# Attention row maxima from half-depth products: two query tiles side by side in the two row halves of the array, one VectorE maximum for both

## The chip, the cores and the metric

The kernel runs on one NeuronCore of a Trainium2 chip. The metric is device time in microseconds (us) for one launch; lower is better. All matrix work is on TensorE (PE), and "weight load" is its LDWEIGHTS (PEld), which the profile lists apart. VectorE is DVE, ScalarE is ACT, GpSimd is POOL, and the queue that issues nearly all transfers is SP.

## The reference

A block of two layers over x of shape (8, 1024, 512): attention (8 heads of 64, biases drawn at random) and then a gated feed-forward layer. Only the attention matters here.

```python
qk = x @ W_qk + b_qk                       # x is layer-normalised before
q, k = qk.reshape(b, s, H, D_HEAD, 2)[..., 0], qk.reshape(...)[..., 1]
v = (x @ W_v + b_v).reshape(b, s, H, D_HEAD)
sim = einsum('bihd,bjhd->bhij', q, k) * D_HEAD ** -0.5
attn = softmax(sim, axis=-1)               # over all 1024 keys j
o = einsum('bhij,bjhd->bihd', attn, v).reshape(b, s, V_DIM)
y = _layernorm(o @ W_out + b_out, ln_gamma, ln_beta)
return (y + x) * RSQRT2
```

## The kernel before

The program has two passes, attention (to about 2,040 us) and then the output projection with the feed-forward layer, which the change does not touch. The attention pass goes through 8 batches of 8 heads, one head at a time. Matmuls that need accuracy take fp32 numbers split into a high part and a low part in the type fp32r.

For each head, `qA` holds the high part of q twice: partitions 0 to 63 come from ACT (L555), and partitions 64 to 127 are a copy made by a DMA (L206). `kA` holds the low part of k in partitions 0 to 63 (DVE, L380) and its high part in 64 to 127 (ACT, L554). `kB` holds a second copy of the high part of k in partitions 0 to 63, by the DMA issued right behind (L207), and a row of ones in partition 64. `qB` holds the low part of q (DVE, L382) and in partition 64 the negated row maxima.

Softmax needs for each query the maximum over all keys before the exponentials are made. So the scores are computed twice:

- "Rows": `rows(b, h, first, end)` on PE (L683 to L701) makes 16 products of 128 queries by 512 keys, each over 128 partitions (q high times k low plus q high times k high), into two PSUM banks in turn (`ps_max[0]`, `ps_max[1]`). `reduce_max` on DVE (L389) takes the maximum of each bank. Product j waits for the maximum of product j-2. After the 16th, `join_max` joins the halves, PE turns the 128 x 8 result (L706), ACT copies it out (L560) and a DMA puts it in `qB`.
- "Scores": `scores` (L708 to L722) makes the transposed scores with the maxima already taken off, four matmuls for each of 8 key tiles: L720 over 128 partitions and L721 over 65. ACT takes the exponential (L578), and POOL adds up the probabilities (L305).
- `p_at_v` (L724) multiplies four key tiles of probabilities by v. These matmuls are fp32, each with 64 stationary columns: the two query halves go to the two column halves of the array. `sum_rows` (L737) has the same form.

The order on every engine is written by hand. While head h has its scores and p_at_v, head h+1 has its rows, and the projection of q and k (`project_qk`, two halves of 512 queries with 12 matmuls each, L661) is spread among them: the second half for h+1 early in the head, the first half for h+2 late. There are four kinds of head on PE and DVE: `late_v_head` (place 0, with the second half of v's projections), `plain_head` (places 1 to 5, and place 6 of the last batch), `turning_head` (place 6, with the transposes of the next batch's input) and `early_v_head` (place 7). `begin_head` runs the last four tiles of p_at_v of the head before, `sum_rows` and `turn_max`.

On SP, `copy_qk(b, h+1, half)` waits for ACT's `qk_hi_done` and issues the copy of q and then that of k. In before, `rows` waits for the copy of q (`q_dup_in`) and for DVE's low part of k (`k_lo_done`); only `scores`, a whole head later, waits for the copy of k (`k_dup_in`).

`project_v` of tile t needs the bank `ps_misc` emptied of tile t-1: PE waits in `free_of_v` for DVE's `store_v` (L387), which stands in DVE's order among the maxima.

The PE order of a plain head, 16 products of rows among the rest:

```python
project_qk(b, h + 1, 1, 8, 12); rows(b, h + 1, 2, 3)
scores(b, h, 0, 1); rows(b, h + 1, 3, 4); scores(b, h, 1, 3)
rows(b, h + 1, 4, 6); scores(b, h, 3, 4); rows(b, h + 1, 6, 8)
```

Of the kernel before, what the change touches and what calls it, by code (L numbers as in the profile page):

```python
# [17 lines left out]
F32 = mybir.dt.float32  # L18
# [28 lines left out]
def rows_of(j):  # L47

    if j < 8:
        return j % 4, j // 4  # L50
    return 4 + (j - 8) // 2, j % 2


def attention_pass(nc, x, w_qk, b_qk, w_v, b_v, w_out, w_r, w_out_raw, stage, o_scratch, inv_scratch, ln1_stats, ident):
    with ExitStack() as ctx:
# [48 lines left out]
        ps_max = [ctx.enter_context(nc.psum_tensor(f"ps_max{i}", [P, HALF], F32)) for i in range(2)]  # L104
# [4 lines left out]
        first_turns = [misc4] + [ps[:, :].rearrange("p (k n) -> p k n", k=KC) for ps in (ps_max[0], ps_max[1], ps_o)]  # L109
# [63 lines left out]
        def turn_bank(t):  # L173

            bank = ps_misc if t in (4, 5, 6) else ps_max[1] if t in (1, 3) else ps_max[0]
            return bank[:, :].rearrange("p (k n) -> p k n", k=KC)
# [5 lines left out]
        with nc.Block() as block:  # L182
# [160 lines left out]
            def _(dve):  # L343
# [45 lines left out]
                def reduce_max(b, h, first, end):  # L389

                    for j in range(first, end):
                        r, kh = rows_of(j)
                        dve.wait_ge(rows_done, 128 * b + 16 * h + j + 1)
                        dve.tensor_reduce(half_max[:, r, kh:kh + 1], ps_max[(j + 1) % 2][:, :], AX_X,  # L394
                                          ALU.max).then_inc(max_done, 1)

                def join_max(b, h):

                    dve.wait_ge(max_done, 128 * b + 16 * h + 16)
                    dve.tensor_reduce(neg_max[:, :], half_max[:, :, :], AX_X, ALU.max, negate=True).then_inc(neg_max_done, 1)  # L400
# [20 lines left out]
                for t in range(4):  # L421
                    reduce_max(0, 0, 3 * t, 3 * t + 3)
                    store_v(0, t)
                reduce_max(0, 0, 12, 16)
                join_max(0, 0)

                def plain_head(b, h, last):
# [10 lines left out]
                    reduce_max(b, h + 1, 0, 3)  # L438
                    store_qk_lo(b, h + 1, 1)
                    reduce_max(b, h + 1, 3, 4)  # L440
                    if h >= 1:
                        invert_sums(b, h - 1)
                    reduce_max(b, h + 1, 4, 10)
# [4 lines left out]
                    reduce_max(b, h + 1, 10, 16)  # L448
                    join_max(b, h + 1)

                def late_v_head(b, h):
                    bb = b + h // HEADS
                    store_qk_lo(b, h + 1, 0)
                    reduce_max(b, h + 1, 0, 3)
                    store_qk_lo(b, h + 1, 1)
                    reduce_max(b, h + 1, 3, 4)
                    if h >= 1:
                        invert_sums(b, h - 1)
                    reduce_max(b, h + 1, 4, 7)
                    store_v(bb, 4)  # L460
                    reduce_max(b, h + 1, 7, 9)
                    store_v(bb, 5)
                    reduce_max(b, h + 1, 9, 10)
                    store_v(bb, 6)
                    reduce_max(b, h + 1, 10, 12)
                    store_v(bb, 7)
                    reduce_max(b, h + 1, 12, 16)
                    join_max(b, h + 1)

                def turning_head(b, h):  # L470
# [8 lines left out]
                    reduce_max(b, h + 1, 0, 2)  # L479
                    store_xT_lo(b + 1, 4, turn_bank(4))  # L480
                    reduce_max(b, h + 1, 2, 4)
                    invert_sums(b, h - 1)
                    reduce_max(b, h + 1, 4, 5)
                    store_xT_lo(b + 1, 5, turn_bank(5))
                    reduce_max(b, h + 1, 5, 7)
                    normalise(b + 1, 6)
                    normalise(b + 1, 7)
                    reduce_max(b, h + 1, 7, 16)
                    join_max(b, h + 1)

                def early_v_head(b, h):
# [6 lines left out]
                    reduce_max(b, h + 1, 1, 7)  # L498
                    store_v(b + 1, 0)
                    reduce_max(b, h + 1, 7, 9)  # L500
                    store_v(b + 1, 1)
                    reduce_max(b, h + 1, 9, 11)
                    store_v(b + 1, 2)
                    reduce_max(b, h + 1, 11, 13)
                    store_v(b + 1, 3)
                    reduce_max(b, h + 1, 13, 16)
# [23 lines left out]
                dve.reciprocal(xhat[0][:, :], ps_max[1][:, :]).then_inc(recip_done, 1)  # L530
# [5 lines left out]
            def _(act):  # L536
# [21 lines left out]
                def store_max_row(b, h):  # L558
                    act.wait_ge(max_turned, 8 * b + h + 1)
                    act.activation(max_row[:, :], ps_max[0][0:TT, 0:P], ACT.Copy).then_inc(max_row_done, 1)  # L560

                def store_o(b, h):
# [4 lines left out]
                    act.activation(sums[:, :], ps_max[1][:, :], ACT.Copy).then_inc(sum_copied, 1)  # L567
# [80 lines left out]
            def _(pe):  # L648
# [34 lines left out]
                def rows(b, h, first, end):  # L683

                    for j in range(first, end):
                        r, kh = rows_of(j)
                        if j == 0:
                            pe.wait_ge(q_dup_in[0], 128 * b + 16 * h + 16)
                            pe.wait_ge(k_lo_done, 16 * b + 2 * h + 1)
                            if h >= 2:  # L690
                                pe.wait_ge(sum_copied, 8 * b + h - 1)
                        if j == 1 and h >= 1:
                            pe.wait_ge(max_row_done, 8 * b + h)
                        if j == 4:
                            pe.wait_ge(k_lo_done, 16 * b + 2 * h + 2)
                        if j == 8:
                            pe.wait_ge(q_dup_in[1], 128 * b + 16 * h + 16)
                        if j >= 2:
                            pe.wait_ge(max_done, 128 * b + 16 * h + j - 1)
                        pe.matmul(ps_max[(j + 1) % 2][:, :], qA[h % 2][:, r * P:(r + 1) * P],  # L700
                                  kA[h % 2][:, kh * HALF:(kh + 1) * HALF], start=True, stop=True).then_inc(rows_done, 1)  # L701

                def turn_max(b, h):

                    pe.wait_ge(neg_max_done, 8 * b + h + 1)
                    pe.transpose(ps_max[0][0:TT, 0:P], neg_max[:, :], ident[:, :]).then_inc(max_turned, 1)  # L706
# [30 lines left out]
                def sum_rows(b, h, all_max):  # L737
# [3 lines left out]
                    for half in range(2):  # L741
                        ins = pe.matmul(ps_max[1][half * DH:(half + 1) * DH, :], ones[:, :],
# [15 lines left out]
                for t in range(4):  # L758
                    rows(0, 0, 3 * t, 3 * t + 3)
                    project_v(0, t)  # L760
                rows(0, 0, 12, 14)
                free_of_qk(0, 0, 0)
                project_qk(0, 1, 0, 0, 12)
# [719 lines left out]
```

## Time and profile before

| what | us |
|---|---|
| median of 3 runs | 2854.5 (2852.35 to 2860.09) |
| profiled execution, device time | 2849.87 |
| its span, first to last instruction | 2848.1 |
| PE busy | 2670.5 (94% of the span) |
| DVE busy | 1782.4 (63%) |
| POOL busy | 1425.2 (50%) |
| ACT busy | 1258.6 (44%) |

The profiled execution lies 1.77 us above its own span. Busy time of PE is a union of records whose ends are modelled, so it says only that PE seldom rests; what a matmul really takes is read from the distance between two starts.

### The profile page before, as it was taken

Reading aid. Unit: us, or ns where it says so; the run is one execution under the profiler, and the core shown is the slowest. Engines: PE = TensorE matmul, PEld = TensorE weight load, DVE = VectorE, ACT = ScalarE, POOL = GpSimd, SP = SyncE. Lnnn points to the kernel's source line nnn. Section 1 sums busy time; section 2 is a strip of 40 time slices with the busy share of each in tenths; the row PEclk is TensorE's granted clock in tenths of the full one; section 3 lists DMA queues with packets and bytes.
Section 4 is the critical chain, followed back from the end, with each engine's and each line's share of the span. In section 5 each row is a group of like instructions: output and inputs, shape, how many; then the busy total and the mean of one; then the engine's idle time right before and its main releaser. Section 6 shows DMA issues by size and latency. Waiting matters only on the chain. (4 is left out here: it accounts for less than half of the span.)

```text
span 2848.1 us, 35993 instructions
## 1 busy us (share of the span) xinstructions
PE 2670.5 (94%) x11376; PEld 1800.3 (63%) x11376; DVE 1782.4 (63%) x2761; ACT 1258.6 (44%) x1719; POOL 1425.2 (50%) x738
## 2 busy tenths in 40 slices
PE   5998999999899999989999998999679999999999
PEld 4655655565565566656556565665357777777777
DVE  5556456546645654564565456455388787878785
ACT  2444244334434433443443344344355565556554
POOL 2575466557545655754565565466523333333333
PEclk9999999999999999999999999999889999999999
DMA  3211021121112112111211211112212121212110
GB/s 104 59 38 36 23 72 34 30 64 40 34 25 75 31 30 65 42 34 27 75 31 30 65 42 34 27 45 68 85 53 74 58 75 57 75 57 75 55 64 30
DMA packets 89739, 145.06 MB, mean 51 GB/s; under 512 B 20096, under 2 KB 20608, under 8 KB 89600
## 3 DMA queue, kind: packets, MB, share of 16 engines
q1 hardware_dynamic: 89600, 143.19, 17.6%
q8 instruction: 90, 1.47, 0.2%
q14 instruction: 49, 0.40, 0.0%
HBM read 75.24 MB, written 33.81 MB: 38 GB/s over the span
## 5 line engine op out<-in xcount | busy, mean ns | idle before, releaser
L305 POOL TENSOR_TENSOR acc<-acc,probs 128x1024 f32<-128x1024 f32 x384 | 915.1, 2383 | 215.8 <-ACT probs L578 187.1
L394 DVE TENSOR_REDUCE half_max<-ps_max 128x1 f32<-128x512 f32 x1024 | 678.7, 686 | 517.1 <-PE ps_max L700 511.3
L578 ACT ACTIVATE probs<-ps_st 128x1024 f32<-128x1024 f32 x512 | 522.2, 1024 | 702.4 <-PE ps_st L721 677.0
L732 PE MATMUL ps_o<-probs,v 128*64 128x512 f32 x2048 | 474.2, 605 | 12.9 <-issue 12.9
L301 POOL TENSOR_TENSOR acc<-probs 128x1024 f32<-128x1024 f32 x64 | 157.4, 2460 | 626.4 <-ACT probs L578 626.4
L700 PE MATMUL ps_max<-kA,qA 128*128 128x512 f32 x1024 | 394.6, 425 | 66.3 <-DVE half_max L394 51.1
L720 PE MATMUL ps_st<-qA,kA 128*128 128x512 f32 x1024 | 419.7, 410 | 7.7 <-DMA qB<-max_row 2.4
L721 PE MATMUL ps_st<-qB,kB 65*128 65x512 f32 x1024 | 412.7, 403 | 0.0
L700 PEld LDWEIGHTS ps_max<-kA,qA 128*128 128x128 f32 x1024 | 192.4, 192 | 207.2 <-DVE half_max L394 95.9
L732 PEld LDWEIGHTS ps_o<-probs,v 128*64 128x64 f32 x2048 | 137.4, 138 | 284.5 <-issue 256.2
L720 PEld LDWEIGHTS ps_st<-qA,kA 128*128 128x128 f32 x1024 | 197.4, 193 | 76.0 <-ACT probs L578 33.5
L721 PEld LDWEIGHTS ps_st<-qB,kB 65*128 65x128 f32 x1024 | 197.9, 193 | 41.9
L661 PE MATMUL ps_misc<-xT_hi,wqk_lo 128*128 128x512 f32 x508 | 209.8, 413 | 5.0 <-DVE v L387 2.2
L661 PE MATMUL ps_misc<-xT_lo,wqk_hi 128*128 128x512 f32 x508 | 205.4, 404 | 0.0
L661 PE MATMUL ps_misc<-xT_hi,wqk_hi 128*128 128x512 f32 x508 | 204.6, 403 | 0.0
L554 ACT ACTIVATE kA<-ps_misc,bqk 64x512 fp32r<-64x512 f32 x127 | 86.6, 682 | 228.7 <-PE ps_misc L661 226.2
L387 DVE TENSOR_TENSOR v<-ps_misc,bv 128x512 f32<-128x512 f32 x60 | 41.5, 691 | 187.5 <-PE ps_misc L669 187.5
L380 DVE SCALAR_TENSOR_TENSOR kA<-ps_misc,bqk,kA 64x512 fp32r<-64x512 f32 x127 | 95.9, 755 | 91.1 <-ACT qA L555 73.5
L1385 PE MATMUL bank<-mix_wout_hi,o_lo 128*128 128x512 f32 x256 | 103.5, 404 | 24.1 <-DVE o_lo L1166 14.7
L560 ACT ACTIVATE max_row<-ps_max 8x128 fp32r<-8x128 f32 x64 | 17.1, 268 | 244.0 <-PE ps_max L706 244.0
L661 PEld LDWEIGHTS ps_misc<-xT_hi,wqk_lo 128*128 128x128 f32 x508 | 98.2, 193 | 26.1 <-DVE v L387 5.3
L661 PEld LDWEIGHTS ps_misc<-xT_hi,wqk_hi 128*128 128x128 f32 x508 | 98.5, 194 | 23.4
(166 smaller groups left out, 4539.4 us busy)
## 6 DMA issues: line engine op xcount, KB each, us to landing
stage<-in_L_attn_x_dram SPq DMA_DIRECT2D x32, 512.0 KB, 5.7
qA<-qA SPq DMA_DIRECT2D x128, 128.0 KB, 2.2
kB<-kA SPq DMA_DIRECT2D x128, 128.0 KB, 2.3
o_scratch<-oT SPq DMA_DIRECT2D x128, 128.0 KB, 2.3
stage<-o_scratch SPq DMA_DIRECT2D x16, 1024.0 KB, 5.6
xc<-in_L_attn_x_dram SPq DMA_DIRECT2D x16, 1024.0 KB, 5.4
out_dram<-gate SPq DMA_DIRECT2D x64, 256.0 KB, 2.0
inv_cols<-inv_scratch SPq DMA_DIRECT2D x126, 128.0 KB, 2.8
```

Of the source, the lines that this page charges most:

```text
L301: pool.tensor_tensor(acc[:, :], probs[:, 0, :], probs[:, 1, :], ALU.add).then_inc(acc_done, 1)
L305: pool.tensor_tensor(acc[:, :], acc[:, :], probs[:, j, :], ALU.add).then_inc(acc_done, 1)
L380: dve.scalar_tensor_tensor(kA[i][0:DH, cols], ps[DH:P, :], bqk[DH:P, hd:hd + 1], f32(kA[i][DH:P, cols]), ALU.add, ALU.subtract).then_inc(k ...
L394: dve.tensor_reduce(half_max[:, r, kh:kh + 1], ps_max[(j + 1) % 2][:, :], AX_X, ALU.max).then_inc(max_done, 1)
L554: act.activation(kA[i][DH:P, cols], ps[DH:P, :], ACT.Identity, bias=bqk[DH:P, hd:hd + 1])
L578: act.activation(probs[:, j, :], ps_st[j % 2][:, :], ACT.Exp).then_inc(exp_done, 1)
L661: ins = pe.matmul(ps[:, :], w[:, kc, h % HEADS, :, :].rearrange("p s d -> p (s d)"), xt[:, kc, cols], start=(n == 0), stop=(n == 11))
L700: pe.matmul(ps_max[(j + 1) % 2][:, :], qA[h % 2][:, r * P:(r + 1) * P], kA[h % 2][:, kh * HALF:(kh + 1) * HALF], start=True, stop=True).th ...
L720: pe.matmul(ps_st[j % 2][:, cols], kA[h % 2][:, tile], qA[h % 2][:, cols], start=True, stop=False)
L721: ins = pe.matmul(ps_st[j % 2][:, cols], kB[h % 2][:, tile], qB[h % 2][:, cols], start=False, stop=True)
L732: ins = pe.matmul(ps_o[half * DH:(half + 1) * DH, :], v[:, j, hd * DH:(hd + 1) * DH], probs[:, j, half * HALF:(half + 1) * HALF], start=(j ...
L1385: ins = pe.matmul(out, a[:, kc, a_cols], b[:, kc, b_cols], start=(i == 0), stop=(i == len(prods) - 1))
```

## The change

`rows` no longer makes 16 products over 128 partitions. It makes 8 pairs m = 0 to 7. The two matmuls of a pair take 64 partitions each: the first takes partitions 0 to 63 of `qA` and of `kB` for one query tile, the second partitions 64 to 127 of `qA` and `kA` for the next query tile. Both are q high times k high, so the term q high times k low is no longer in the maximum. They write the two banks of one PSUM tensor, `ps_pair`, and one DVE instruction takes both maxima (128 x 2 x 512 in, 128 x 2 out). Pair m waits for the maximum of pair m-1. The waits on `k_lo_done` become waits on `k_dup_in`. In each kind of head the calls are placed anew, on PE and on DVE.

```diff
-def rows_of(j):
-    if j < 8:
-        return j % 4, j // 4
-    return 4 + (j - 8) // 2, j % 2
+def rows_of(m):
+    if m < 4:
+        return 2 * (m % 2), m // 2
+    return 4 + 2 * ((m - 4) // 2), m % 2
...
-        ps_max = [ctx.enter_context(nc.psum_tensor(f"ps_max{i}", [P, HALF], F32)) for i in range(2)]
+        ps_pair = ctx.enter_context(nc.psum_tensor("ps_pair", [P, 2, HALF], F32))
+        ps_max = [ps_pair[:, i, :] for i in range(2)]
...
 def reduce_max(b, h, first, end):
-                    for j in range(first, end):
-                        r, kh = rows_of(j)
-                        dve.wait_ge(rows_done, 128 * b + 16 * h + j + 1)
-                        dve.tensor_reduce(half_max[:, r, kh:kh + 1], ps_max[(j + 1) % 2][:, :], AX_X,
-                                          ALU.max).then_inc(max_done, 1)
+                    for m in range(first, end):
+                        r, kh = rows_of(m)
+                        dve.wait_ge(rows_done, 64 * b + 8 * h + m + 1)
+                        dve.tensor_reduce(half_max[:, r:r + 2, kh], ps_pair[:, :, :], AX_X, ALU.max).then_inc(max_done, 1)
...
-                def rows(b, h, first, end):
+                def rows(b, h, m):
+                    r, kh = rows_of(m)
+                    if m == 0:
+                        pe.wait_ge(q_dup_in[0], 128 * b + 16 * h + 16)
+                        pe.wait_ge(k_dup_in[0], 128 * b + 16 * h + 16)
+                        if h >= 2:
+                            pe.wait_ge(sum_copied, 8 * b + h - 1)
+                        if h >= 1:
                             pe.wait_ge(max_row_done, 8 * b + h)
-                        if j == 4:
-                            pe.wait_ge(k_lo_done, 16 * b + 2 * h + 2)
-                        if j == 8:
-                            pe.wait_ge(q_dup_in[1], 128 * b + 16 * h + 16)
-                        if j >= 2:
-                            pe.wait_ge(max_done, 128 * b + 16 * h + j - 1)
-                        pe.matmul(ps_max[(j + 1) % 2][:, :], qA[h % 2][:, r * P:(r + 1) * P],
-                                  kA[h % 2][:, kh * HALF:(kh + 1) * HALF], start=True, stop=True).then_inc(rows_done, 1)
+                    if m == 2:
+                        pe.wait_ge(k_dup_in[1], 128 * b + 16 * h + 16)
+                    if m == 4:
+                        pe.wait_ge(q_dup_in[1], 128 * b + 16 * h + 16)
+                    if m >= 1:
+                        pe.wait_ge(max_done, 64 * b + 8 * h + m)
+                    cols = slice(kh * HALF, (kh + 1) * HALF)
+                    pe.matmul(ps_pair[:, 0, :], qA[h % 2][0:DH, r * P:(r + 1) * P], kB[h % 2][0:DH, cols],
+                              start=True, stop=True)
+                    pe.matmul(ps_pair[:, 1, :], qA[h % 2][DH:P, (r + 1) * P:(r + 2) * P], kA[h % 2][DH:P, cols],
+                              start=True, stop=True).then_inc(rows_done, 1)
```

The order on PE in the new plain head (the pair numbers are the last arguments of `rows`; project_qk calls are in groups of four matmuls):

```python
project_qk(b, h + 1, 1, 0, 4); rows(b, h + 1, 0); project_qk(b, h + 1, 1, 4, 8)
project_qk(b, h + 1, 1, 8, 12); rows(b, h + 1, 1); scores(b, h, 0, 1); scores(b, h, 1, 3)
rows(b, h + 1, 2); scores(b, h, 3, 4); rows(b, h + 1, 3)
free_of_qk(b, h + 1, 1); project_qk(b, h + 2, 0, 0, 4); scores(b, h, 4, 5)
rows(b, h + 1, 4); scores(b, h, 5, 6); p_at_v(b, h, 0)
rows(b, h + 1, 5); scores(b, h, 6, 7); rows(b, h + 1, 6)
project_qk(b, h + 2, 0, 4, 8); scores(b, h, 7, 8); project_qk(b, h + 2, 0, 8, 12)
rows(b, h + 1, 7)
```

In the late_v head DVE now has `reduce_max` of pair 5 ahead of `store_v(bb, 6)`, where before it had products 10 and 11 behind it:

```diff
-                    reduce_max(b, h + 1, 7, 9)
+                    reduce_max(b, h + 1, 4, 5)
                     store_v(bb, 5)
-                    reduce_max(b, h + 1, 9, 10)
+                    reduce_max(b, h + 1, 5, 6)
                     store_v(bb, 6)
-                    reduce_max(b, h + 1, 10, 12)
+                    reduce_max(b, h + 1, 6, 7)
                     store_v(bb, 7)
-                    reduce_max(b, h + 1, 12, 16)
+                    reduce_max(b, h + 1, 7, 8)
```

and PE there has `scores(5)`, `p_at_v`, `free_of_v(5)`, `project_v(6)`, `rows(5)`, `scores(6)`, `free_of_v(6)`, `project_v(7)`, `rows(6)`, `scores(7)`, `rows(7)`, `free_of_v(7)`. In the turning head DVE's maximum of pair 3 stands behind `normalise` of tiles 6 and 7, and PE has `rows(3)`, `p_at_v`, `rows(4)`. In the early_v head pair 0 is moved behind `scores(0)`, and the last pair ahead of `free_of_v(3)` and the projection. The prologue places its pairs in the same way.

## Rows read from the trace of the kernel before

**Rows 1.** The page: busy time, and the granted clock in 40 slices.

```profile
PE 2670.5 (94%) x11376; PEld 1800.3 (63%) x11376; DVE 1782.4 (63%) x2761; ACT 1258.6 (44%) x1719; POOL 1425.2 (50%) x738
...
PEclk9999999999999999999999999999889999999999
```

**Rows 2.** Groups of instructions, shapes apart: busy us, mean ns of one | idle before.

```profile
L394 DVE TENSOR_REDUCE half_max<-ps_max 128x1 f32<-128x512 f32 x1024 | 678.7, 686 | 517.1 <-PE ps_max L700 511.3
L700 PE MATMUL ps_max<-kA,qA 128*128 128x512 f32 x1024 | 394.6, 425 | 66.3 <-DVE half_max L394 51.1 <-ACT inv_cols L567 8.9 <-DVE xT_lo L373 3.2
...
L1166 DVE TENSOR_TENSOR o_lo<-stage,o_hi 128x2048 fp32r<-128x2048 f32 x16 | 36.5, 2283 | 0.0
...
L1211 DVE TENSOR_TENSOR mr_lo<-stage,mr_hi 128x512 fp32r<-128x512 f32 x64 | 40.8, 698 | 0.0
```

**Rows 3.** Timeline of a late_v head: start us, duration us, engine, instruction.

```profile
837.23 0.40 PE L721 MATMUL ps_st<-qB,kB 65*128 65x512 f32 x1
...
837.47 0.39 PE L700 MATMUL ps_max<-kA,qA 128*128 128x512 f32 x1
...
837.78 0.20 PEld L732 LDWEIGHTS ps_o<-probs,v 128*64 128x64 f32 x4 [0.36 <-issue]
837.79 3.65 PE L732 MATMUL ps_o<-probs,v 128*64 128x512 f32 x16
837.89 0.69 DVE L394 TENSOR_REDUCE half_max<-ps_max 128x1 f32<-128x512 f32 x1 [0.47 <-PE ps_max L700]
838.27 0.14 PEld L732 LDWEIGHTS ps_o<-probs,v 128*64 128x64 f32 x2 [0.29 <-issue]
...
840.41 0.14 PEld L732 LDWEIGHTS ps_o<-probs,v 128*64 128x64 f32 x2 [0.28 <-issue]
841.37 0.19 PEld L669 LDWEIGHTS ps_misc<-wv_hi,xT_lo 128*128 128x128 f32 x1 [0.81 <-issue]
841.37 0.50 PE L669 MATMUL ps_misc<-wv_hi,xT_lo 128*128 128x512 f32 x1
841.48 0.19 PEld L669 LDWEIGHTS ps_misc<-wv_lo,xT_hi 128*128 128x128 f32 x1
841.71 0.40 PE L669 MATMUL ps_misc<-wv_lo,xT_hi 128*128 128x512 f32 x1
```

**Rows 4.** Timeline of a plain head, from the end of its projection on.

```profile
861.27 0.39 PE L661 MATMUL ps_misc<-xT_hi,wqk_hi 128*128 128x512 f32 x1
...
862.39 0.69 ACT L555 ACTIVATE qA<-ps_misc,bqk 64x512 fp32r<-64x512 f32 x1
...
863.66 0.59 SPq L207 DMA_DIRECT2D kB<-kA  x1
...
864.03 0.19 PEld L720 LDWEIGHTS ps_st<-qA,kA 128*128 128x128 f32 x1 [0.48 <-ACT probs L578]
...
864.84 0.19 PEld L700 LDWEIGHTS ps_max<-kA,qA 128*128 128x128 f32 x1
...
865.29 0.19 PEld L700 LDWEIGHTS ps_max<-kA,qA 128*128 128x128 f32 x1 [0.26 <-DVE half_max L394]
```

**Rows 5.** The DMA of L207: landing after issue, us.

```profile
DMA to landing us min/median/max: 2.3/2.3/4.0
```

**Rows 6.** Who waited for whom: us in total, times, longest.

```profile
PEld ps_max L700 <- DVE half_max L394: 95.9, 138, 5.9
...
PE ps_max L700 <- DVE half_max L394: 51.1, 18, 5.4
```

**Rows 7.** Stretches of an early_v head: PE, PEld, DVE, ACT, POOL busy, granted clock, DMA.

```profile
785.00:790.00 5.00, 3.61 (x15) 2.41 (x14) 3.98 (x6) 2.74 (x4) 3.12 (x2) 1.00 0.25 53
790.00:794.00 4.00, 4.00 (x13) 2.05 (x13) 1.39 (x2) 2.05 (x2) 3.92 (x2) 0.57 0.26 70
```

More of the change, by code:

```diff
@@ L566, in store_o @@
                         act.wait_ge(o_done, 8 * b + h)
[L567 removed]
+                    act.activation(sums[:, :], ps_max[1], ACT.Copy).then_inc(sum_copied, 1)
                     act.wait_ge(pv_done, 8 * b + h + 1)
@@ L741, in sum_rows @@
                     for half in range(2):
-                        ins = pe.matmul(ps_max[1][half * DH:(half + 1) * DH, :], ones[:, :],
+                        ins = pe.matmul(ps_pair[half * DH:(half + 1) * DH, 1, :], ones[:, :],
                                         acc[:, half * HALF:(half + 1) * HALF], start=True, stop=True)
@@ L758, in _ @@
                 for t in range(4):
-                    rows(0, 0, 3 * t, 3 * t + 3)
+                    rows(0, 0, t)
                     project_v(0, t)
-                rows(0, 0, 12, 14)
+                rows(0, 0, 4)
                 free_of_qk(0, 0, 0)
-                project_qk(0, 1, 0, 0, 12)
-                rows(0, 0, 14, 16)
+                project_qk(0, 1, 0, 0, 6)
+                rows(0, 0, 5)
+                project_qk(0, 1, 0, 6, 12)
+                rows(0, 0, 6)
+                rows(0, 0, 7)
                 def begin_head(b, h):
@@ L828, in late_v_head @@
                     scores(b, h, 4, 5)
-                    rows(b, h + 1, 7, 9)
+                    rows(b, h + 1, 4)
                     free_of_v(bb, 4)
@@ L832, in late_v_head @@
                     scores(b, h, 5, 6)
-                    rows(b, h + 1, 9, 10)
                     p_at_v(b, h, 0)
@@ L836, in late_v_head @@
                     project_v(bb, 6)
-                    rows(b, h + 1, 10, 12)
+                    rows(b, h + 1, 5)
                     scores(b, h, 6, 7)
@@ L864, in turning_head @@
                     free_of_xhat(b + 1, 3)
-                    rows(b, h + 1, 0, 2)
+                    rows(b, h + 1, 0)
                     free_of_qk(b, h + 1, 1)
@@ L911, in early_v_head @@
                     project_v(b + 1, 0)
-                    rows(b, h + 1, 7, 9)
+                    rows(b, h + 1, 4)
                     scores(b, h, 5, 6)
@@ L915, in early_v_head @@
                     project_v(b + 1, 1)
-                    rows(b, h + 1, 9, 11)
+                    rows(b, h + 1, 5)
                     scores(b, h, 6, 7)
@@ L919, in early_v_head @@
                     project_v(b + 1, 2)
-                    rows(b, h + 1, 11, 13)
+                    rows(b, h + 1, 6)
                     scores(b, h, 7, 8)
```

120 lines of the change are left out of this document (48 added, 72 removed).

## The prediction

> **What bounds the kernel now.** I read the page first. PE is busy 94% of the span, no other engine over 63% [rows 1], and the granted clock is near full in every slice. Then the groups [rows 2]: the row products and their maxima are the two lines that the change rewrites. DVE sits idle 517 us before the maxima, nearly all of it waiting for PE, so a cheaper maximum buys nothing by itself. Last the timelines, where the distance between starts counts. In the run of 128-column fp32r matmuls one takes 0.23 us (841.48 to 841.71) [rows 3]. The attention pass is a chain of such slots on PE with few holes, so the time after is PE's slots plus PE's holes. L700 waited for DVE 147 us in all [rows 6], part of it under a running matmul.
>
> **The row products, if a pair ran at its best.** 1024 products of 0.23 us are 238 us. 512 pairs at one slot each would be 119 us: a gain of 0.23 us a pair, or 1.86 us a head. Whether that comes depends on two things the trace doesn't show for row halves: do both matmuls stream together, and does the array pass freely from whole depth to half depth and back?
>
> The nearest row is p_at_v, which splits the array by columns. Its 16 matmul records take 3.65 us, and a new pair of weight loads starts every 0.43 us (838.27 to 840.41 is five steps) [rows 3]. Two matmuls do run side by side. But the way in and out costs. In: the product of L700 starts at 837.47, so its slot ends at 837.70; the next load starts only at 837.78 and the pair at 838.27 - 0.43 = 837.84, so 0.14 us are lost, of which 0.06 is a load of 64 columns laid bare. Out: the last pair starts at 840.41 + 0.43 = 840.84 and ends at 841.27; the load starts at 841.37 and streaming at 841.48: 0.21 us lost, with 0.11 for 128 columns. With 128-column loads both ways a switch costs about 0.19 to 0.21, say 0.195 us.
>
> The other end is zero. L721 takes 65 partitions of 128 and follows and precedes L720 and L700 without a hole (837.23, 837.47) [rows 3]. But its 65 partitions don't fit a half of the array, so it is no proof that a half-depth matmul is free. I take the switching price, because the new matmuls, like p_at_v, divide the array so that two fit, and L721 doesn't. The Trainium skill ("TensorEngine Tiling (Array Packing)", Tiling Modes, Key Properties) says that changing the tiling mode, not just the tile, drains TensorE. By that rule the half-depth pair pays a drain on each side, as p_at_v does here; without it the sum would be that of the first rival. The trace agrees for columns and shows no case of rows.
>
> Then a pair between whole-depth matmuls costs 0.23 + 2 x 0.195 = 0.62 us against 0.46 before: 0.16 us more. Where one side touches p_at_v, that side's switch was paid already: 0.43 against 0.46, 0.04 less. By the new orders, pairs touching p_at_v are 2 in each of 41 plain heads, 3 in each of 7 turning heads, 1 in each of 7 early_v heads: 110. The other 402 cost 64 us, the 110 give back 4: **+60 us**. Bounds: 512 x -0.23 = -118 us with no drain, and +55 us more (512 x 0.11) if the second load of each pair waits for the first; p_at_v's four loads fall in 0.20 us, so I take them as parallel.
>
> **The wait on the copy of k.** Pair 2 needs `k_dup_in[1]`, where product 4 needed only DVE's low part. Take a plain head and let P = 861.27 be the start of the projection's last matmul [rows 4]. ACT finishes at 863.08, SP issues q's copy and then k's at 863.66, and it lands 2.3 us later [rows 5]: P + 4.69, and some 0.05 to the load. On PE: pair 1 starts at P + 0.43 (slot and switch), scores at P + 0.85, the third scores tile waits for ACT as before (load 864.03, so start P + 2.87), its last matmul is at P + 3.57, and pair 2's load could start at P + 3.89. So PE stands 0.85 us. The next product's load before was at 864.84, already P + 3.57, with the copy still 1.1 us away. Behind this waiting load PE holds scores 3, hence ACT's exponentials, and p_at_v; nothing later in the head has slack on PE to take it up. The late_v head has the same beginning. 49 heads x 0.85: **+42 us**. In turning and early_v heads pair 2 comes later or behind a DVE wait of about the same length. Pair 0 waits for `k_dup_in[0]`, issued about 4 us before; that is free. q's copies were waited for before.
>
> **One buffer instead of two.** Pair m waits for maximum m-1. The new maximum has 1024 elements: from 698 ns at 512 and 2283 ns at 2048 columns [rows 2] one column costs 1.03 ns, so 686 + 512 x 1.03 = 1.21 us. A cycle from load to load: the matmul is over 0.50 us after an exposed load (841.37, 0.50) [rows 3], DVE starts 0.04 us later (837.47 + 0.39 to 837.89), 1.21 us, and 0.05 to PE: 1.81 us. PE's other work between two pairs with n matmuls between fills 0.42 + 0.11 + 0.23n - 0.02 + 0.10, so 1.53 us at n = 4 and 2.47 at n = 8. With n = 4 PE stands 0.28 us. That happens twice in a plain head (pairs 2 to 3 and 5 to 6), once more in the last batch's place 6, twice in late_v (2 to 3, 6 to 7) and twice in turning (2 to 3, 4 to 5): 113 x 0.28 = **+32 us**, and 1 us in the prologue, where pairs 6 and 7 touch. Everywhere else the gap covers it. DVE's own saving (1.21 against two of 0.69 that overlap to about 1.28) is nothing on PE.
>
> **Places on DVE.** In late_v, `store_v` of tile 6 now stands behind the maximum of pair 5. That makes it end 0.54 + 1.13 + 0.69 = 2.37 us after pair 5's load, and PE wants to load for the projection of tile 7 at 1.23 us: 1.1 us late, and some 0.1 at tile 7: 8 heads, **+9 us**. In turning heads pair 4 waits for the maximum of pair 3 behind two `normalise`, 1.3 us, where products 9 and 10 waited 0.65: **+5 us**. Early_v heads lose a wait of 0.4 us behind the last `store_v`: **-3 us**.
>
> **Waits that go.** Back-to-back products in plain heads wait for the maximum two back (865.29 against 865.07 in the free run) [rows 4]: 0.1 to 0.13 us twice and 0.09 at product 0. About 0.3 us in 41 heads and 0.1 in 8: **-13 us**.
>
> **The clock.** A hole can cost more than itself. In the early_v head PE stood 1.7 us before 788.03, and in the stretch from 790 to 794 the granted clock is 0.57 [rows 7], that is about 3.4 us at 1.2 GHz instead of 2.4, which costs 1.7 us. Not every hole did that. The new holes are about 0.9 to 1.1 us. If each of the 49 waits for k drew such a stretch it would be 83 us; if none, nothing. The turning and early_v holes that drew it before stay. I take four new stretches: **+7 us**.
>
> **Sum.** 60 + 42 + 32 + 1 + 9 + 5 - 3 - 13 + 7 = 140. The profiled execution was 2849.9 us, 4.6 below the median of the runs, so 2990. This is 135 us above the median.
>
> **The rivals.**
>
> *No drain.* The pair streams in one slot and costs nothing at the edges. For it: L721's clean passage [rows 3]. Against it: p_at_v's. Then pairs give 118 us back, but PE arrives sooner at both waits: k's copy is 1.34 us away (49 heads, 66 us), and a cycle of 1.82 us between starts meets 0.24 + 0.93 us of work, 0.65 us missing at 113 places (73 us). With 26 for late_v and the other places and -13: +34, so 2884 us. The Trainium skill ("TensorE: Matmul & The Clock Gate", Part 3, Packing small matmuls) has matmuls in distinct row groups start some 4 ns apart. It speaks for the concurrency on which forecast and this rival both build, and says nothing there of what stands around the pair.
>
> *Faster.* The same free pair, and the copy of k is there when pair 2 asks. Place: between L207's landing and pair 2's load. Then the 66 us fall away: -118 + 73 + 26 - 13 = -32, so 2818 us. It decides as soon as a head's new waits are under 1.86 us; in the plain head they are 1.34 + 1.30. Against it: the landing at P + 4.69 hangs on ACT and a 2.3 us transfer, neither of which the change touches.
>
> *Drain, and no full overlap.* Loads one behind the other: 2990 + 55 = 3045. Matmuls one behind the other as well (512 x 0.21 = 109): 3099.
>
> *The change doesn't do what it says.* No drain and no concurrency: 1024 slots as before, k's wait 1.1 us (54), single buffer 0.66 at 113 places (75), 26 and -13: +142, so 2992. It gives the same time as the forecast by another way; the profile would tell them apart.
>
> *Clock.* The new holes draw many slow stretches: up to 83 us more, 3070.
>
> **Chances.** Forecast 0.62; no drain 0.14; faster 0.03; drain without full overlap 0.11; no concurrency and no drain 0.07; clock 0.03. Predicted time 2990. The forecast's own range, with k's wait from 0.6 to 1.1 us and switches from 0.17 to 0.21 us, is 2955 to 3030. The range for 8 in 10 reaches down to the no-drain case and up over the serial loads: 2880 to 3065. What this measurement can tell from no change is 0.3%, about 8.6 us. Faster 0.03, same 0.02 (the no-drain case with half its waits), slower 0.95.
>
> **What would show it.** After: the two matmuls of a pair start within about 10 ns; from a matmul before the pair to the pair's load 0.31 us, and from the pair to the next load again 0.31; an idle PE of 0.8 us before pair 2 in plain heads, ended by the DMA kB<-kA; idle ended by DVE half_max at pairs 3 and 6; a maximum of 1.21 us; a plain head of 28.0 us instead of 26. If the load after a pair starts with the pair, the drain is wrong and the time is near 2884. If the second matmul starts a slot later, concurrency is wrong. If pair 2 is not held by the copy, 42 us are gone.

## Result and profile after

The changed kernel takes **2961.16 us** (2958.14 to 2968.37), against 2853.43 for the kernel before: +107.7 us, ratio **1.0376 [1.035, 1.0402]**. It is slower, as forecast, by 108 us where the forecast had 135. Its profiled span is 2961.5 us, 113.4 more than before; that is what the rows below add up to.

The page after, against [rows 1] and [rows 2]:

```profile
PE 2726.2 (92%) x11376; PEld 1692.5 (57%) x11376; DVE 1716.5 (58%) x2249; ACT 1259.4 (43%) x1719; POOL 1422.4 (48%) x738
...
PEclk9999999999999999999998999999979999999999
...
L395 DVE TENSOR_REDUCE half_max<-ps_pair 128x2 f32<-128x1024 f32 x512 | 626.5, 1224 | 764.7 <-PE ps_pair L699 763.7
...
L697 PE MATMUL ps_pair<-kB,qA 64*128 64x512 f32 x512 | 256.8, 502 | 100.8 <-DVE half_max L395 53.8
...
L699 PE MATMUL ps_pair<-kA,qA 64*128 64x512 f32 x512 | 258.3, 505 | 0.0
```

PE is busy 56 us longer and idle 58 us longer. DVE saves 52 us on the maxima (626.5 against 678.7) and waits 248 us longer for them (764.7 against 517.1): its saving buys nothing. L699 never has an idle time before it, since it starts with L697.

The clearest measure is the distance from one `turn_max` (the 8-row transposes of L706, after L705) to the next, one for each head. Worked out from their starts, mean of the heads of one place, us:

| place | 0 late_v | 1 | 2 | 3 | 4 | 5 | 6 turning | 7 early_v |
|---|---|---|---|---|---|---|---|---|
| before | 37.62 | 28.28 | 25.94 | 25.99 | 25.98 | 33.23 | 29.51 | 42.38 |
| after | 41.10 | 29.72 | 27.92 | 27.86 | 27.87 | 32.20 | 31.15 | 46.15 |
| times heads | +27.8 | +11.5 | +15.8 | +15.0 | +15.1 | **-8.2** | +13.1 | +26.4 |

With -3.4 before the first `turn_max` that is 113 (us, in the profiled executions). After the last one both kernels take 834.1 us. (Place 6 holds the last batch's plain head too, and place 7 has 7 distances.)

A plain head after, from the last matmul of its projection on, as in [rows 4]: start, duration, engine, instruction.

```profile
902.50 0.40 PE L658 MATMUL ps_misc<-xT_hi,wqk_hi 128*128 128x512 f32 x1
902.83 0.49 PE L697 MATMUL ps_pair<-kB,qA 64*128 64x512 f32 x1
902.83 0.49 PE L699 MATMUL ps_pair<-kA,qA 64*128 64x512 f32 x1
903.25 0.50 PE L719 MATMUL ps_st<-qA,kA 128*128 128x512 f32 x1
903.59 0.39 PE L720 MATMUL ps_st<-qB,kB 65*128 65x512 f32 x1
...
905.65 0.50 PE L719 MATMUL ps_st<-qA,kA 128*128 128x512 f32 x1 [0.25 <-ACT probs L575]
...
907.38 0.49 PE L697 MATMUL ps_pair<-kB,qA 64*128 64x512 f32 x1 [0.54 <-DMA kB<-kA]
907.39 0.50 PE L699 MATMUL ps_pair<-kA,qA 64*128 64x512 f32 x1
...
909.20 0.50 PE L697 MATMUL ps_pair<-kB,qA 64*128 64x512 f32 x1 [0.17 <-DVE half_max L395]
```

and PE's weight loads at the first pair:

```profile
902.83 0.18 PEld L697 LDWEIGHTS ps_pair<-kB,qA 64*128 64x128 f32 x1 [0.37 <-issue]
902.83 0.18 PEld L699 LDWEIGHTS ps_pair<-kA,qA 64*128 64x128 f32 x1
903.25 0.19 PEld L719 LDWEIGHTS ps_st<-qA,kA 128*128 128x128 f32 x1 [0.24 <-issue]
903.36 0.19 PEld L720 LDWEIGHTS ps_st<-qB,kB 65*128 65x128 f32 x1
```

The reader sees three things. The pair is one slot: both matmuls and both loads start together. It is fenced off on both sides: 0.33 us from the start of the matmul before to the pair's load, 0.42 from there to the next load, which is bare, that is, under no running matmul (the one behind it comes 0.11 later, when streaming begins). So the pair costs 903.36 - 902.50 - 0.23 = 0.63 us, where two products cost 0.46. And the pair at 907.38 waits for the copy of k, the one at 909.20 for the maximum of the pair before it.

### The profile page after: what moved, and what is told of

It is laid out like the page before. It is cut to its first block and busy times, and to the rows that moved or that the text cites. A ratio compares the mean times of both kernels' runs of the same rounds, so it can differ in the third digit from the quotient of the medians.

```text
span 2961.5 us, 34367 instructions
## 1 busy us (share of the span) xinstructions
PE 2726.2 (92%) x11376; PEld 1692.5 (57%) x11376; DVE 1716.5 (58%) x2249; ACT 1259.4 (43%) x1719; POOL 1422.4 (48%) x738
## 5 line engine op out<-in xcount | busy, mean ns | idle before, releaser
L395 DVE TENSOR_REDUCE half_max<-ps_pair 128x2 f32<-128x1024 f32 x512 | 626.5, 1224 | 764.7 <-PE ps_pair L699 763.7
L731 PE MATMUL ps_o<-probs,v 128*64 128x512 f32 x2048 | 481.2, 613 | 10.5 <-issue 10.5
L719 PE MATMUL ps_st<-qA,kA 128*128 128x512 f32 x1024 | 449.0, 438 | 27.0 <-ACT probs L575 14.6
L697 PE MATMUL ps_pair<-kB,qA 64*128 64x512 f32 x512 | 256.8, 502 | 100.8 <-DVE half_max L395 53.8
L697 PEld LDWEIGHTS ps_pair<-kB,qA 64*128 64x128 f32 x512 | 94.9, 185 | 324.9 <-issue 186.8
L699 PE MATMUL ps_pair<-kA,qA 64*128 64x512 f32 x512 | 258.3, 505 | 0.0
L658 PE MATMUL ps_misc<-xT_hi,wqk_lo 128*128 128x512 f32 x508 | 219.1, 431 | 6.0 <-DVE v L388 2.5
L658 PE MATMUL ps_misc<-xT_lo,wqk_hi 128*128 128x512 f32 x508 | 218.0, 429 | 0.0
L658 PEld LDWEIGHTS ps_misc<-xT_lo,wqk_hi 128*128 128x128 f32 x508 | 99.7, 196 | 38.1 <-issue 24.5
L557 ACT ACTIVATE max_row<-ps_pair 8x128 fp32r<-8x128 f32 x64 | 17.1, 267 | 238.7 <-PE ps_pair L705 238.7
```

The source lines that it names most:

```text
L395: dve.tensor_reduce(half_max[:, r:r + 2, kh], ps_pair[:, :, :], AX_X, ALU.max).then_inc(max_done, 1)
L658: ins = pe.matmul(ps[:, :], w[:, kc, h % HEADS, :, :].rearrange("p s d -> p (s d)"), xt[:, kc, cols], start=(n == 0), stop=(n == 11))
L697: pe.matmul(ps_pair[:, 0, :], qA[h % 2][0:DH, r * P:(r + 1) * P], kB[h % 2][0:DH, cols], start=True, stop=True)
L699: pe.matmul(ps_pair[:, 1, :], qA[h % 2][DH:P, (r + 1) * P:(r + 2) * P], kA[h % 2][DH:P, cols], start=True, stop=True).then_inc(rows_done, 1)
L719: pe.matmul(ps_st[j % 2][:, cols], kA[h % 2][:, tile], qA[h % 2][:, cols], start=True, stop=False)
L731: ins = pe.matmul(ps_o[half * DH:(half + 1) * DH, :], v[:, j, hd * DH:(hd + 1) * DH], probs[:, j, half * HALF:(half + 1) * HALF], start=(j ...
```

## The experiments

Ratios are against the kernel before, timed again with each group of runs: 2852.41 us (half_depth, depth_96, before_k_wait, pair_no_copy), 2855.19 (pair_short_max, pair_k_first and the two spread kernels of experiment 4) and 2855.23 (the last two kernels). Time at the lower clock is added up from the clock records of each kernel's profiled execution; at half the clock, half of such time is lost where PE is busy.

**1. What does half depth cost by itself?** Two kernels made from before. In the first each product uses the upper 64 partitions alone, one at a time; the second takes 96 partitions, which no half of the array can hold.

```diff
-pe.matmul(ps_max[(j + 1) % 2][:, :], qA[h % 2][:, r * P:(r + 1) * P],
-          kA[h % 2][:, kh * HALF:(kh + 1) * HALF], ...)
+pe.matmul(ps_max[(j + 1) % 2][:, :], qA[h % 2][DH:P, r * P:(r + 1) * P],     # half_depth
+          kA[h % 2][DH:P, kh * HALF:(kh + 1) * HALF], ...)
+pe.matmul(ps_max[(j + 1) % 2][:, :], qA[h % 2][0:96, r * P:(r + 1) * P],     # depth_96
+          kA[h % 2][0:96, kh * HALF:(kh + 1) * HALF], ...)
```

> The kernel before with one edit: each of the 16 row products takes only partitions 64 to 127 of qA and kA (q high times k high, so the low part of k is left out of the maxima), one matmul at a time, two buffers and all waits as before. It tells what a half-depth matmul costs by itself. Theory (the array drains on each change between whole and half depth, 0.39 us for a group of products between whole-depth matmuls, 0.195 for one that touches p_at_v): 12 groups in a plain head, about 4.3 us a head, some of it taken up by waits that are there already: 3070 to 3110 us. Rival (half depth is free, as L721's 65 partitions are): 2853 us.

> The kernel before with the row products over partitions 0 to 95 instead of 0 to 127 (the rest of the sum is left out of the maxima). Theory: what costs is the division of the array and not the smaller depth, and 96 partitions don't fit a half, so nothing changes: 2853 us. Rival (any depth below 128 drains): near half_depth's time.

Measured: half depth 3089.68 us, ratio 1.0821 [1.0805, 1.0836], +237 us; a plain head takes 29.55 us instead of 25.98. With 96 partitions 2861.53 us, 1.0031 [1.0018, 1.0043]: all heads of places 0 to 6 keep their length to 0.25 us, and the early_v heads grow (44.28 against 42.38 us, times 7 = 13), by more time at the lower clock (41 us in the seven heads against 14). Of the 237 us of half_depth some 55 are the clock too (245 us at the lower level against 135), but the plain heads of places 2 to 4 have no such time in either kernel, so their 3.6 us are the passages. The loads of half_depth around a group of two products, and the matmuls before and behind it:

```profile
720.93 0.19 PEld L721 LDWEIGHTS ps_st<-qB,kB 65*128 65x128 f32 x1
721.16 0.40 PE L721 MATMUL ps_st<-qB,kB 65*128 65x512 f32 x1
721.49 0.29 PEld L700 LDWEIGHTS ps_max<-kA,qA 64*128 64x128 f32 x2 [0.37 <-issue]
...
722.15 0.19 PEld L720 LDWEIGHTS ps_st<-qA,kA 128*128 128x128 f32 x1 [0.37 <-issue]
...
722.50 0.40 PE L721 MATMUL ps_st<-qB,kB 65*128 65x512 f32 x1
```

From 721.16 to 722.50 are 1.34 us, with four slots of 0.23 in them: 0.41 us lost around the group. Around the pair it is 0.39 (902.50 to 903.59, three slots), so the loss belongs to the two passages and not to what stands between them.

What follows: 65 rows [rows 3] and 96 rows cost nothing at the passage, 64 rows do. Other numbers of rows were not tried. The number of products and the waits are the same in both kernels. No drain, as three of the rivals had it, is out. The Trainium skill ("TensorEngine Tiling (Array Packing)", Tiling Modes, Key Properties) has every change of the tiling mode drain TensorE; the trace now agrees for rows as well as for columns.

**2. The wait for the copy of k.** Put into before, where nothing needs it; taken out of after by reading the low part of k in `kA`, which DVE writes without a transfer; and made shorter in after by issuing k's copy ahead of q's.

```diff
+                            pe.wait_ge(k_dup_in[0], 128 * b + 16 * h + 16)    # before_k_wait, j == 0
+                            pe.wait_ge(k_dup_in[1], 128 * b + 16 * h + 16)    # before_k_wait, j == 4
...
-                        pe.wait_ge(k_dup_in[0], 128 * b + 16 * h + 16)        # pair_no_copy, m == 0
+                        pe.wait_ge(k_lo_done, 16 * b + 2 * h + 1)
-                        pe.wait_ge(k_dup_in[1], 128 * b + 16 * h + 16)        # pair_no_copy, m == 2
+                        pe.wait_ge(k_lo_done, 16 * b + 2 * h + 2)
-pe.matmul(ps_pair[:, 0, :], qA[h % 2][0:DH, r * P:(r + 1) * P], kB[h % 2][0:DH, cols], ...)
+pe.matmul(ps_pair[:, 0, :], qA[h % 2][0:DH, r * P:(r + 1) * P], kA[h % 2][0:DH, cols], ...)
...
-                    sp.dma_start(f32(qA[i][DH:P, cols]), f32(qA[i][0:DH, cols])).then_inc(q_dup_in[half], 16)   # pair_k_first
                     sp.dma_start(f32(kB[i][0:DH, cols]), f32(kA[i][DH:P, cols])).then_inc(k_dup_in[half], 16)
+                    sp.dma_start(f32(qA[i][DH:P, cols]), f32(qA[i][0:DH, cols])).then_inc(q_dup_in[half], 16)
```

> The kernel before, with the waits of products 0 and 4 extended by the wait for the copy of k (k_dup_in), as the change has them. Theory: product 4's load moves from 3.57 to 4.74 us behind the projection's last matmul, 1.2 us in 42 heads (the plain heads but place 5, where a later hole of 5 us takes it up, and late_v), less 0.1 for a wait that is there: about +45, 2898 us. Rival (hidden): 2853 us.

> The changed kernel, but the first matmul of each pair reads kA's partitions 0 to 63 (the low part of k) instead of kB's, so that pairs wait for k_lo_done and not for the copy of k; the maxima of half of the tiles are of another product. Forecast's price of the wait: 0.85 us in 49 heads, 2919 us. By the trace of the changed kernel part of that stands behind a later exponential, and place 5 takes its share up: 0.61 us in 42 heads, about 2933 us. Rival (the wait costs nothing): 2961 us.

> The changed kernel with SP issuing the copy of k ahead of that of q. k lands 0.56 us earlier. Theory: 0.56 us in 42 heads, about 2938 us. Rival (pair 2 is held by something else): 2961 us.

Measured: before_k_wait 2888.83 us (1.0122 [1.0107, 1.0137]), +36. pair_no_copy 2940.91 us (1.0302 [1.0289, 1.0316]), 20.3 less than after. pair_k_first 2940.43 us (1.0304 [1.0288, 1.032]), 20.7 less. All three moved less than expected, though the expectations had left place 5 out: at place 5 the heads did not stay as they were but went the other way. With the copy taken out the plain head falls from 27.87 to 27.37 us, but place 5 rises from 32.20 to 33.80, 12.8 us over 8 heads; with k first it rises to 33.58; with the wait put into before it falls from 33.23 to 30.96. What happens there is shown under experiment 4. In the early_v heads of pair_no_copy the time at the lower clock fell from 55 to 38 us, which is most of the 9.5 us gained there; the places 0 to 4, where the wait is, gained 22.8. In pair_k_first the copy is hardly waited for any more. Releasers of L697 in the changed kernel (us in total, times):

```profile
  DVE half_max L395: 182.9, 259
...
  DMA kB<-kA: 44.4, 64
```

and the same list of pair_k_first:

```profile
  DMA kB<-kA: 2.6, 7
```

Half a microsecond in a plain head is all that the wait was worth, not 0.85: the third scores tile, the last but one ahead of pair 2 (905.65), already waits 0.25 us for ACT's exponential, so without the copy pair 2 could load at 905.65 + 0.11 + 3 x 0.23 + 0.31, about 906.77, at the soonest, against 907.38.

**3. The single buffer.** Half as many columns for the maximum in after, so that the next pair is let in sooner.

```diff
-dve.tensor_reduce(half_max[:, r:r + 2, kh], ps_pair[:, :, :], AX_X, ALU.max).then_inc(max_done, 1)
+dve.tensor_reduce(half_max[:, r:r + 2, kh], ps_pair[:, :, 0:HALF // 2], AX_X, ALU.max).then_inc(max_done, 1)
```

> The changed kernel with a maximum over half of each bank's columns (128 x 2 x 256 in place of 128 x 2 x 512; the other columns are left out). DVE's part of the one-buffer cycle goes from 1.22 to about 0.69 us. Theory: the stalls of 0.25 us where four matmuls stand between two pairs go (some 106 places, 26 us) and half a microsecond at late_v's store_v (4 us): about 2931 us. Rival (one buffer costs nothing, or DVE's rate is of no matter): 2961 us.

Measured: 2938.23 us (1.0289 [1.0272, 1.0306]), 22.9 less than after. The plain head falls by 0.51 us, the late_v head by 1.10, and place 5 rises by 1.25 us, which gives back 10. The early_v heads give back another 7.8, by more time at the lower clock (72 us against 55). The places 0 to 4 and 6 gained 39 us together.

**4. What stands at place 5.** Half of DVE's work for the next batch's input, and the copy of its statistics, moved away from the front of that head, in before and in after alike.

```diff
                     if extra and place == 5:
-                        keep_stats(b + 1)
-                        for t in range(4):
+                        dve.wait_ge(rstd_done, b + 2)
+                        for t in range(2):
                             normalise(b + 1, t)
...
                     join_max(b, h + 1)
+                    if extra and place == 5:
+                        for t in range(2, 4):
+                            normalise(b + 1, t)
...
                     store_qk_lo(b, h + 1, 0)
+                    keep_stats(b + 1)
```

> The kernel before with the DVE work of place 5 moved: two of its four normalise stay ahead of maximum 10, two go behind join_max, and keep_stats goes into the turning head. In the trace of before PE stands 5.1 us ahead of product 12 in 7 heads, each followed by a stretch at the lower clock. Theory: the hole goes, 7 x 5.1 us and about 12 us of clock, 2805 to 2815 us. Rival (the work only moves to another hole of DVE that PE waits for): 2840 to 2853 us.

> The changed kernel with the same DVE work moved in the same way. Theory (why the forecast was 30 us too high: in place 5 the pairs' costs went into a hole that DVE makes anyway): without that hole the change costs more than its 108 us, so the distance to before_spread is 125 to 140 us, about 2940 us. Rival (the forecast's terms were too large everywhere): the distance stays near 108 us.

Measured: before_spread **2806.86 us**, ratio 0.9834 [0.9819, 0.9849]; place 5 takes 26.31 us instead of 33.23, place 6 30.79 instead of 29.51. pair_spread 2934.73 us, 1.0277 [1.026, 1.0293]; place 5 27.95 us instead of 32.20. Between the two lie **127.9 us**, not 107.7. The hole at place 5 had paid 20 us of the change. By place, before_spread gained 55 us at place 5, of which 24 are the clock (48 us at the lower level, none now), and lost 10 at place 6. That its 48 us are what was expected (36 for the holes and 12 for the clock) is luck in part. Of the 127.9 us some 20 are the clock (118 us at the lower level in pair_spread, 78 in before_spread).

Before at place 5, PE's row and then DVE's:

```profile
736.76 0.80 PE L700 MATMUL ps_max<-kA,qA 128*128 128x512 f32 x1 [5.38 <-DVE half_max L394]
```

```profile
726.27 1.69 DVE L361 COPY ln_stats<-mean_var 128x8 f32 x1
727.95 8.16 DVE L367 TENSOR_SCALAR xhat<-stage,mean_var,rstd 128x512 f32<-128x512 f32 x4
736.03 0.68 DVE L394 TENSOR_REDUCE half_max<-ps_max 128x1 f32<-128x512 f32 x1
```

and after, the same:

```profile
772.57 0.50 PE L697 MATMUL ps_pair<-kB,qA 64*128 64x512 f32 x1 [2.90 <-DVE half_max L395]
```

```profile
764.59 0.68 DVE L362 COPY ln_stats<-mean_var 128x8 f32 x1
765.26 6.12 DVE L368 TENSOR_SCALAR xhat<-stage,mean_var,rstd 128x512 f32<-128x512 f32 x4
771.30 1.21 DVE L395 TENSOR_REDUCE half_max<-ps_pair 128x2 f32<-128x1024 f32 x1
```

PE stood 5.38 us behind DVE's copy, four `normalise` and a maximum, and stands 2.90 after. DVE's block in front of the maximum is 3.05 us shorter (764.59 to 771.30 against 726.27 to 736.03): the copy takes 0.68 us instead of 1.69 and the four `normalise` 6.12 instead of 8.16. Their lengths go with POOL's additions. A `normalise` that starts while an addition of probabilities runs ends about 0.3 us after it, some 2.6 us in all; one that starts beside none takes 0.53. With the copy of k taken out of after, the block starts sooner, and so does POOL's next addition, at 760.28:

```profile
755.05 8.14 DVE L368 TENSOR_SCALAR xhat<-stage,mean_var,rstd 128x512 f32<-128x512 f32 x4
763.11 1.21 DVE L395 TENSOR_REDUCE half_max<-ps_pair 128x2 f32<-128x1024 f32 x1
...
760.28 2.62 POOL L306 TENSOR_TENSOR acc<-acc,probs 128x1024 f32<-128x1024 f32 x1 [0.32 <-ACT probs L575]
...
764.37 0.79 PE L697 MATMUL ps_pair<-kA,qA 64*128 64x512 f32 x1 [5.38 <-DVE half_max L395]
```

The fourth `normalise` now starts 0.34 us behind that addition, where in after it started 0.12 us ahead of it, and PE stands 5.38 us again. The same head (the third batch) in six kernels, us from its `turn_max`, read from the starts and durations:

| kernel | block starts | `normalise` that met an addition | block ends | mean of place 5 |
|---|---|---|---|---|
| before | 12.89 | 3 of 4 | 22.72 | 33.23 |
| before_k_wait | 14.05 | 2 | 20.71 | 30.96 |
| after | 14.33 | 2 | 21.12 | 32.20 |
| pair_no_copy | 13.86 | 3 | 23.13 | 33.80 |
| pair_k_first | 13.84 | 3 | 23.13 | 33.58 |
| pair_short_max | 13.56 | 3 | 23.13 | 33.45 |

So this hole is no fixed time that takes up the cost. One addition more or less is worth 2 us here, and which it is hangs on a few tenths of a microsecond.

**5. Only the switches left.** pair_spread with the edits of pair_no_copy and pair_short_max, and in the late_v head the maximum of pair 5 behind `store_v` of tile 6. It stands against before_spread.

```diff
                     store_v(bb, 5)
-                    reduce_max(b, h + 1, 5, 6)
                     store_v(bb, 6)
-                    reduce_max(b, h + 1, 6, 7)
+                    reduce_max(b, h + 1, 5, 7)
                     store_v(bb, 7)
```

> pair_spread with every wait taken away that the change added: the first matmul of a pair reads kA's low part (no wait for the copy of k), the maximum takes half of the columns (short cycle), and in late_v heads store_v of tile 6 stands ahead of the maximum of pair 5. The maxima are of other numbers. What is left of the change is its matmuls. Theory: against before_spread (2806.9 us) the switches cost 60 us and 13 us of waits are gone: 2845 to 2870 us, and a plain head of 26.6 us against 25.98. Rival (without its waits the pair gains, because it saves a slot): under 2807 us.

Measured: 2839.36 us (0.9942 [0.9928, 0.9956]), **32.5 us above before_spread** and 95.4 below pair_spread. So of the 127.9 us the switches, less the waits that go, are 33, and the waits for k, for the single buffer and for `store_v` are 95. Both hold some clock: 7 us of the 33 (91 us at the lower level against 78) and 14 of the 95. Between the two profiled executions the 33 are 41 (spans of 2839.6 and 2798.3 us), since that of before_spread lay 7 us under its median. The plain head takes 26.84 us against 25.99 of before_spread; I had expected 26.6. The sum fell below the expected range (2845 to 2870) since the time before the first `turn_max` is 5.5 us shorter (58.7 against 64.2) and place 1 0.57 us a head.

**6. A faster version.** before_spread, and in the early_v head two maxima ahead of the second `store_qk_lo`:

```diff
                     invert_sums(b, h - 1)
+                    reduce_max(b, h + 1, 1, 3)
                     store_qk_lo(b, h + 1, 1)
-                    reduce_max(b, h + 1, 1, 7)
+                    reduce_max(b, h + 1, 3, 7)
```

> before_spread, and in the early_v head DVE takes maxima 1 and 2 ahead of the second store_qk_lo instead of behind it. In before PE stands 1.46 us ahead of product 3 there, and a stretch at the lower clock follows in some of the 7 heads. Theory: about 0.6 to 1 us of each hole goes, and some of those stretches: 2787 to 2802 us. Rival (product 4 then waits for the low part of k as long): 2807 us.

Measured: **2789.56 us**, ratio 0.9769 [0.9756, 0.9783], place 7 40.81 us instead of 42.16. Between the profiled executions it is 10.8 us ahead of before_spread, 9.5 of them at place 7, where no time at the lower clock is left (10 us before); the medians lie 17 us apart. It is the fastest of all kernels here, 65.7 us ahead of the kernel before, and computes all that the reference asks.

## Why the prediction was right, and where its sizes were off

The direction, the mechanism and the order of size were right: forecast +140 for the sum, 135 over the median, +107.7 measured, with 127.9 once the hole of place 5 is out of both kernels. Step by step:

**Switches (+60, with -13 for waits that go and +1 in the prologue).** Right in kind: 0.63 us for a pair, forecast 0.62. Together 33 us measured (pair_drains_only) against 48, or 41 between the profiled executions. A plain head has somewhat more than forecast (+0.85 us against 6 x 0.16 - 2 x 0.04 - 0.3 = 0.6), but the prologue gives back 5.5 us. There in before the products waited for DVE four times, 4.4 us in all and up to 1.69 us at a time; after has one such wait, of 1.32 us. Why place 1 becomes shorter was not found.

**Wait for k (+42).** Right in place, too large. The landing was forecast at P + 4.74 for the load and was P + 4.88 (902.50 to 907.38). Failed step: "the third scores tile waits for ACT as before"; its load was forecast at P + 2.76 and came at P + 3.15, since ACT's exponentials follow scores tiles that are themselves late, and behind it PE arrives later at pair 2, so that 0.5 us a plain head could be had back and not 0.85. Taking the copy away gave 20.3 us in all; the places 0 to 4 gave 22.8, where the forecast has 34 for these 40 heads.

**One buffer (+32).** As forecast: a cycle of 909.20 - 907.38 = 1.82 us (1.81), a maximum of 1.224 us (1.21). The price of a column came from TENSOR_TENSOR rows, another instruction; that it holds for the maximum was not known beforehand. Halving the maximum gave 22.9 us in all, and 39 without places 5 and 7, more than the 32 forecast: the late_v and the place-1 heads have 20 of them (1.10 and 1.42 us each), the others 0.5 to 0.7, forecast 0.56.

**late_v's `store_v` (+9), turning heads (+5), early_v (-3), clock (+7).** The first is there, 0.78 us of idle time and some 0.95 us late where 1.1 was forecast:

```profile
886.18 0.50 PE L666 MATMUL ps_misc<-wv_hi,xT_lo 128*128 128x512 f32 x1 [0.78 <-DVE v L388]
```

Places 0 and 6 came to 27.8 and 13.1 us, forecast 30 and 15 with their shares of the switches. Place 7 came to 26.4 us, where its switches less the 3 us were 5, and the clock 7. The wait at pair 2 was judged rightly ("behind a DVE wait of about the same length"): PE stood there for DVE before, stands 0.7 us longer for the copy of k after, and with the copy taken out stands for DVE again. (The 1.7 us of the prediction are the idle time of the weight loads; the matmuls stood 1.30.) Before, after and pair_no_copy:

```profile
788.04 1.10 PE L700 MATMUL ps_max<-kA,qA 128*128 128x512 f32 x2 [1.30 <-DVE half_max L394]
...
1089.64 0.49 PE L697 MATMUL ps_pair<-kB,qA 64*128 64x512 f32 x1 [1.98 <-DMA kB<-kA]
...
1081.39 0.50 PE L697 MATMUL ps_pair<-kA,qA 64*128 64x512 f32 x1 [1.65 <-DVE half_max L395]
```

The step that failed is the clock: "The turning and early_v holes that drew it before stay. I take four new stretches". The clock falls behind that hole in all seven heads after, in four of seven before, and for longer. Two stretches of this head (PE, PEld, DVE, ACT, POOL busy, granted clock, DMA):

```profile
1079.00:1090.00 11.00, 8.96 (x30) 6.00 (x30) 4.20 (x6) 4.68 (x6) 2.34 (x1) 0.84 0.22 48
1090.00:1098.00 8.00, 8.00 (x24) 3.60 (x24) 2.45 (x2) 2.05 (x2) 7.06 (x3) 0.57 0.12 33
```

PE is busy in all of the 8 us from 1090 on, at a mean of 0.57 of full speed, so for most of them at 1.2 GHz and not at 2.4. The seven heads spend 55 us at the lower level, against 14 before, which costs 20 us more. Before, a head of 41.5 us has no such time and one of 43.0 has 3.4 us of it; after, one of 44.1 has 3.4 and one of 47.3 has 10.2. Without it a head would take about 42.4 against 41.5 us: 6 us in seven heads, where the forecast had 5. Over the span the lower level took 159 us against 135, so the clock is +12 and not +7; place 5 gave 5 back. What makes the stretches more frequent is open: depth_96 lengthened these heads by 1.9 us in the mean (41 us at the lower level) without any new wait.

**The missed step.** The forecast counted place 5 as one more plain head, +2.0 us. It took -1.0. That is 24 of the 27 us between the sum of 140 and the 113.4 of the spans, and by the experiments it is 20. The other misses nearly cancel (+14 at place 7, -15 elsewhere), and that is luck. The rows were there to be read: the longest of L700's waits for DVE are 5.9 and 5.4 us [rows 6]. The prediction says nothing of where they stand. The 3.0 us a head are those by which DVE's block became shorter, since it met POOL's additions at another moment (experiment 4); that this went in favour of the change is luck too.

**The rivals.** "Faster" and "no drain" fell with the 0.33 and 0.42 us at each side of the pair and with half_depth (the 26 us that they carry for late_v and other places are not worked out in the prediction, and the forecast's own terms there add up to 11); "no full overlap" with the two loads at 902.83; "no concurrency" with the matmuls 3 ns apart (median of all pairs); "clock" was there with 12 us of its bound of 83, 20 of them at place 7 and -5 at place 5. The measured time lies within the own range of the forecast (2955 to 3030), near its lower end.

## What to carry to other kernels

A matmul over half the rows is not a cheap matmul: price what stands before and behind it, and group such matmuls so that many share one passage; a lone pair between whole-depth matmuls loses 0.17 us here. Before costs are summed over like heads, look for the heads in which the engine already stands for something else, and ask what sets the end of that hole: here it was which of DVE's instructions met one of POOL's, so that a saving of half a microsecond elsewhere made the hole 2 us longer. The longest single wait of a busy engine can be worth more than a cleverer instruction: moving four DVE instructions (two `normalise` and the two copies of `keep_stats`) gained 48 us, where the new products lost 108.

## What the runs showed of the hardware beyond that

**DVE beside POOL.** Three of the four `normalise` instructions of place 5 in before end just behind POOL's additions. POOL:

```profile
725.56 9.81 POOL L305 TENSOR_TENSOR acc<-acc,probs 128x1024 f32<-128x1024 f32 x4
```

The four additions of this row end at 727.93, 730.38, 732.88 and 735.37, and DVE's at 727.96 (the copy), 730.66, 733.17 and 735.65. So the first three `normalise` take 2.7, 2.5 and 2.5 us and the fourth, with POOL done, 0.5; the copy of 8 columns takes 1.69 us here and 0.15 in before_spread, where it stands elsewhere. The Trainium skill ("SBUF — State Buffer", Who interferes with whom) has DVE and GpSimd share a port pair that one of them locks while the other is held up; the trace agrees with these numbers. No run takes the additions away: that POOL holds DVE up is read from the table of experiment 4, where it fits in all six kernels. The row maxima, which read PSUM, have 686 ns in the mean [rows 2] although POOL is busy half the span.

**Half-depth matmuls in a row.** In half_depth the second product of a group starts 0.335 us behind the first, where 0.235 is the distance between two products under way. That is no price of two half-depth matmuls in a row: the first record begins with its bare load of 0.11 us, as at 903.25 to 903.59 between whole-depth matmuls. The passage costs 0.41 us around such a group and 0.39 around a pair, so the more half-depth matmuls share one passage, the less each pays.

**The two matmuls of a pair** start 3 ns apart in the median; the Trainium skill ("TensorE: Matmul & The Clock Gate", Part 3, Packing small matmuls) has about 4 ns, and the trace agrees.
